# A fused attention and mixture-of-experts layer on one core: values one key tile at a time, shared-expert products in the odd steps, and two orders turned round

## The reference

```python
def holo_linear(x, basis, phase, amp):
    resonance = jnp.einsum('bli,hi->blh', x, basis)
    w = amp * jnp.cos(phase)
    return jnp.einsum('blh,oh->blo', resonance, w)
...
    attn = jnp.einsum('bhqd,bhkd->bhqk', q, k) * scale
    attn = jax.nn.softmax(attn, axis=-1)
    out = jnp.einsum('bhqk,bhkd->bhqd', attn, v)
    out = out.transpose(0, 2, 1, 3).reshape(Bsz, Ls, C)
    return holo_linear(out, basis_o, phase_o, amp_o)
...
    return jax.nn.silu(x @ wg) * (x @ wu) @ wd          # the shared expert
...
x = L0_attn_x
xn = _layernorm(x, axis=-1)
x = x + _L0_attn_ref(xn, ...) + _L0_ffn_ref(xn, ...)
```

## Time and profile before

| | |
|---|---|
| median of 3 runs | 955.16 us (954.87 to 955.76) |
| the profiled execution | 955.04 us, of which the profile's span is 953.2 us |
| TensorE matmul busy | 869.6 us, 91% of the span |
| VectorE, ScalarE, GpSimd busy | 615.2, 577.1 and 402.1 us |
| mean granted TensorE clock | 0.968 of full speed |

### The profile page before, as it was taken

How to read it: one execution, slowest core, us unless ns; L and a number is a source line. 1 busy time by engine, 2 the same in 40 slices (tenths; PEclk the granted TensorE clock), 3 DMA queues, 4 the chain that set the end, 5 groups by cost and what they waited for, 6 DMA issues and landing times.

```text
span 953.2 us, 19558 instructions
## 1 busy us (share of the span) xinstructions
PE 869.6 (91%) x6491; PEld 607.5 (64%) x6492; DVE 615.2 (65%) x923; ACT 577.1 (61%) x935; POOL 402.1 (42%) x411
## 2 busy tenths in 40 slices
PE   4755899999999989889999999999999999999996
PEld 2435899999999976455555556555555555455462
DVE  7788844344434455776786686786786786786752
ACT  4746644444444452766766666766766766766764
POOL 2003322222222151752753752762753753753841
PEclk9865999999999999999999999999999999999998
DMA  9993655222222217454765764765765755745310
GB/s 304 393 287 137 214 151 169 75 72 74 69 69 74 66 48 182 147 169 107 196 177 121 191 179 111 199 181 117 201 172 125 195 173 126 193 132 120 90 39 32
DMA packets 91480, 140.04 MB, mean 147 GB/s; under 512 B 17512, under 2 KB 51824, under 8 KB 89488
## 3 DMA queue, kind: packets, MB, share of 16 engines
q1 hardware_dynamic: 84720, 121.24, 45.2%
q0 software_dynamic: 6480, 17.70, 6.9%
q10 hardware_dynamic: 208, 0.14, 0.1%
HBM read 79.24 MB, written 54.71 MB: 141 GB/s over the span
## 4 chain that ended last, share of the span: by engine, by line
PE 71%; DVE 13%; DMA 7%; issue 3%; SPq 3%; ACT 3%; POOL 0%; DVEq 0%; ACTq 0%
PE bank L1414 9%; PE bank L1454 9%; PE bank L1313 8%; PE s_pair L1366 7%; PE s_pair L1295 7%; PE bank L1519 7%; PE st_pair L1295 6%; DVE top L1886 5%; PE st_pair L1442 5%; DMA r_rows<-low_rank_rows 5%; PE bank L1303 2%; PE bank L1278 2%; PE bank L1427 1%; PE bank L1468 1%; SPq L558 1%
## 5 line engine op out<-in xcount | busy, mean ns | idle before, releaser
L1886 DVE TENSOR_REDUCE top<-s_pair 128x2 f32<-128x1024 f32 x248 | 303.7, 1225 | 141.5 <-PE s_pair L1366 138.0
L1083 ACT ACTIVATE prob<-st_pair 128x1024 f32<-128x1024 f32 x252 | 258.7, 1027 | 123.7 <-PE st_pair L1442 116.8
L756 POOL DMA_INDIRECT xg<-xn_rows,token_of x71 | 73.0, 1028 | 219.6 <-PE bank L1278 168.4
L1414 PE MATMUL bank<-xT_b,w_sh 64*128 64x512 f32 x960 | 144.1, 406 | 0.5
L1366 PE MATMUL s_pair<-k_rows,q_rows 48*128 48x512 f32 x496 | 115.3, 458 | 12.5 <-DVE top L1886 12.3
L1454 PE MATMUL bank<-prob,v_ones 128*32 128x512 f32 x1024 | 123.1, 598 | 0.0
L1414 PEld LDWEIGHTS bank<-xT_b,w_sh 64*128 64x128 f32 x960 | 92.2, 189 | 31.6 <-issue 8.3
L1442 PE MATMUL st_pair<-q_rows,k_rows 50*128 50x512 f32 x504 | 106.3, 416 | 3.4 <-ACT prob L1083 2.5
L1313 PE MATMUL bank<-w_exp,c_hT 128*128 (+1 forms) x639 | 94.2, 292 | 0.6 <-ACT c_y L995 0.6
L1366 PEld LDWEIGHTS s_pair<-k_rows,q_rows 48*128 48x128 f32 x496 | 47.5, 185 | 64.0 <-DVE top L1886 54.3
L794 POOL TENSOR_TENSOR ao<-ao,o_sum 128x512 f32<-128x512 f32 x15 | 19.3, 1286 | 161.2 <-DMA o_sum<-inverse_rows 161.2
(11 more groups left out here) (230 smaller groups left out, 1269.1 us busy)
## 6 DMA issues: line engine op xcount, KB each, us to landing
qk_rows<-qk_hi SPq DMA_DIRECT2D x56, 256.0 KB
q_rows<-qk_rows SPq DMA_DIRECT2D x64, 192.0 KB
k_rows<-qk_rows SPq DMA_DIRECT2D x56, 192.0 KB
expert_rows<-c_y SPq DMA_DIRECT2D x71, 128.0 KB, 1.7
xn_T_split<-x_T SPq DMA_DIRECT2D x8, 1024.0 KB, 6.5
xT_b<-xn_T_split SPq DMA_DIRECT2D x7, 1024.0 KB, 8.8
qk_rows<-qk_lo SPq DMA_DIRECT2D x28, 256.0 KB
x_all<-in_L_attn_x_dram SPq DMA_DIRECT2D x8, 512.0 KB, 8.2
```

The lines of the kernel that those rows point to most:

```text
L756: pool.indirect_dma_start(xg[s % 4][:, :], None, xn_dram, bass.IndirectOffsetOnAxis(token_of[:, s:s + 1], 0)).then_inc(c_x[s % 4], 16)
L1083: act.activation(prob[n % 3][:, 2 * jp:2 * jp + 2, :].rearrange("p j l -> p (j l)"), score_T_pair(b, g, t)[:, :], ACT.Exp, scale=HD ** -0. ...
L1414: ins = pe.matmul((g_bank, u_bank)[up][:, :], w_sh[rows, a, o:o + P], xT_of(b)[rows, c, k, :], start=(n == 0 and i == 0), stop=(n == 1 and ...
L1886: dve.tensor_reduce(top[g % 2][:, :, jp, qt], score_pair(b, g, v)[:, :].rearrange("p (i k) -> p i k", i=2), AX_X, ALU.max).then_inc(d_max, 1)
```

## The change

The change moves work within the pipeline; nothing is computed otherwise.

1. `values` is issued for one key tile in each even step: key tile 3 of the slot before at t = 0, tiles 0, 1 and 2 at t = 2, 4 and 6. Before it came in twos, at t = 0 and t = 4. The semaphore `b_pv` counts every key tile.
2. A gate/up tile has two pieces of six products, at t % 4 = 1 and 3. Before it had 5, 1, 1 and 5, with the single ones at t % 4 = 2 round `small`. A down product has pieces of 12, 5, 12 and 5, at t % 4 = 1, 2, 3 and 0, in place of 10, 5, 5, 12 and 2, and its banks swap once in place of twice.
3. `score_T` comes ahead of `score` in every step. Before this held for t % 4 = 0 alone.
4. `load_low_rank` is issued ahead of `load_rows`.

```diff
@@ SyncE @@
                 if there(nb):
                     load_max(nb, ng)
+                if g == 3 and there(b + 2):
+                    load_low_rank(b + 2)
                 if there(rb):
                     load_rows(rb, rg)
-                if g == 3 and there(b + 2):
-                    load_low_rank(b + 2)
...
             def slot_first():
                 load_max(0, 0)
                 store_low_rank(1)
+                load_low_rank(1)
                 load_rows(0, 2)
-                load_low_rank(1)
@@ ScalarE @@
-                wait(act, b_pv, (b - 1) * 8 + (half + 1) * 4)
+                wait(act, b_pv, (b - 1) * 16 + (half + 1) * 8)
...
-                    wait(act, b_pv, (n - 3) // 2 + 1)
+                    wait(act, b_pv, n - 2)
...
-                wait(act, b_pv, b * 8 + g * 2 + 2)
+                wait(act, b_pv, b * 16 + g * 4 + 4)
@@ TensorE @@
-            CUTS = (0, 5, 6, 7, 12)
-            DOWN_CUTS = (0, 10, 15, 20, 32, 34)
+            CUTS = (0, 6, 12)
...
-                if kt % 2:
-                    ins.then_inc(b_pv, 1)
+                ins.then_inc(b_pv, 1)
...
-            FROM_LAST = len(DOWNS) - 2
-            DOWN_ORDER = [(0, i) for i in range(FROM_LAST)] + [(1, i) for i in range(len(DOWNS))] + [(0, i) for i in range(FROM_LAST, len(DOWNS))]
+            DOWN_ORDER = [(n, i) for n in range(2) for i in range(len(DOWNS))]
+            DOWN_CUTS = (0, 12, 17, 29, 34)
...
-            def piece(b, g, t, n):
+            def piece(b, g, t):
                 what, c, j = unit(b, g, t // 4) if t % 4 else unit_before(b, g, t // 4)
-                if t % 4 == 0:
-                    if what == "down":
-                        down_pair(c, j, 4)
-                elif what == "pair":
-                    gate_up_shared(c, j, n)
...
+                if what == "down":
+                    down_pair(c, j, (t - 1) % 4)
+                elif what == "pair" and t % 2:
+                    gate_up_shared(c, j, t % 4 // 2)
...
                 for t in range(STEPS):
-                    if t % 4:
-                        next_score(b, g, t)
                     if now:
                         score_T(b, g, t)
+                    next_score(b, g, t)
                     if t % 4 == 0:
-                        next_score(b, g, t)
-                        piece(b, g, t, 4)
+                        piece(b, g, t)
                     if t == 0 and there(pb):
-                        values(pb, pg, 2)
                         values(pb, pg, 3)
-                    if t == 4 and now:
-                        values(b, g, 0)
-                        values(b, g, 1)
+                    elif t % 2 == 0 and t:
+                        values(b, g, t // 2 - 1)
...
             low_rank_o(LAST, (0,))
-            values(LAST, 3, TPB - 2)
             values(LAST, 3, TPB - 1)
```

More of the change, by code:

```diff
@@ L1506, in down_pair @@
                         wait(pe, d_res, b)
-                if piece in (2, 4):
-                    pe.wait_ge(b_ha, swaps(b, SFT + 2 * pair) + piece // 2)
+                if piece == 2:
+                    pe.wait_ge(b_ha, swaps(b, SFT + pair) + 1)
                 for m in range(first, end):
@@ L1649, in _ @@
             pe.wait_ge(c_hed, NS)
-            for n in range(3):
-                gate_up_shared(0, 0, n)
+            gate_up_shared(0, 0, 0)
             score(0, 1, 1)
-            gate_up_shared(0, 0, 3)
+            gate_up_shared(0, 0, 1)
             score(0, 1, 2)
@@ L1656, in _ @@
             score(0, 1, 3)
-            for n in range(4):
+            for n in range(2):
                 gate_up_shared(0, 1, n)
```

27 lines of the change are left out of this document (10 added, 17 removed).

## The result

| | before | after |
|---|---|---|
| median | 955.62 us (952.11 to 959.23, 20 runs) | 959.80 us (955.49 to 966.68, 20 runs) |
| ratio | | 1.0047, interval 1.0032 to 1.0061 |
| profiled execution, span | 955.04, 953.2 us | 958.77, 956.9 us |
| TensorE matmul busy | 869.6 us, 91% | 865.0 us, 90% |
| mean granted TensorE clock | 0.968 | 0.964 |

A forecast was written before the change was run, and what follows sets the result against it. TensorE was taken as the engine others wait for, with its own waits small (46.8 us ahead of score pairs, 7.7 for `r_rows`). Terms +2.0 - 1.6 - 7.7 - 2.0 - 1.5 = -10.8 us from 955.04 gave 944, range 938 to 953.5.

The forecast's parts named there:

- the clash: VectorE's split cast beside GpSimd's `normalise`, end of half 2: `normalise` would start some 0.5 behind the cast, gaining 1.6 us.
- the last slot: End of sequence 7, bound by exponentials: one key tile ahead of the last exponential, worth 0.5 plus about 1.0: -1.5 us.
- low-rank rows: TensorE's waits for `r_rows`: with these loads issued ahead, the seven loads' waits fall away, -7.7 us.
- steps, seven sequences: Halves of a sequence sum to -0.45 - 0.03 + 0.45 + 0.3 = +0.3 us, or +2 for seven sequences.
- held step: t = 0 or 4 behind a pair half: ScalarE's exponential holds the next transposed pair, 2.28 us between bounds 2.2 and 2.4.
- The pair half: Four steps in the new order, 2.00, 1.92, 2.00 and 2.28, sum 8.20 us; halves 0 and 1 gain 0.45.
- rivals of dearer or cheaper held steps: Dearer (12%): 2.4 and products wait 0.1 more, +9, 953 us. Cheaper (10%): 2.1 and odd steps 1.9, some -9, 935.
- The odd half: Half 3, bound by VectorE: 9.33 us before, 9.78 new, a loss of 0.45 as TensorE idles.
- Down halves: Halves 4 to 7: 34.96 us before, 35.27 together after, a loss of 0.3; down half 4 at 8.83.
- More switches: Tiling-mode changes from `values` to a projection: no drain beyond 0.01 seen; by the drain rule, 50 changes, +5 us, 949.
- the slower rival: Casts held beside GpSimd (10%): each 1.0 hold costs 0.97, 24 places, +23 us, 967; from 12 on it decides.
- the 8% rival of a new wait: Waits for `r_rows` stay (8%): the low half's store or the engines' traffic takes their place, 952 us.

The follow-up runs named there:

- experiment 4: Changed kernel with ScalarE's exponential ahead of `up_half` at t = 0 and 4 behind a pair half: 957.64 us, ratio 1.0032.
- experiment 5: Changed kernel with `values` in twos again in the last slot of the last sequence: 959.50 us, ratio 1.0052.
- experiment 1: Kernel before with only the low-rank loads moved ahead: 947.88 us, ratio 0.9938; changed kernel with the old load order: 962.99 us, 1.0085.
- steps alone: Changed kernel with the low-rank loads back behind `load_rows`, so only the step changes remain: 962.99 us, ratio 1.0085.
- spread in one half: New order in half 1 alone, on the kernel before with low-rank loads ahead: 944.35 us; the same with the new product pieces everywhere: 944.64 us.
- GpSimd told to wait: Changed kernel with GpSimd's `normalise` and experts' sum waiting until `split_max` is done: 958.81 us, ratio 1.0039.
- split away from GpSimd: Changed kernel with four small `tensor_reduce` and a `memset` in place of the maxima split's cast and subtraction: 955.81 us, ratio 1.0004.

## Why the prediction was wrong

I predicted -10.8 us; the profiled execution shows +3.7. More than half of the miss of 14.5 is one term, the clash (8.0); the last slot has 3.0 and the steps 2.5. Term by term, with two terms that the prediction did not have. Prices of steps are from the sequences without a clash:

| term | predicted | measured | from |
|---|---|---|---|
| low-rank rows | -7.7 | -7.9 | the six waits of the kernel before, 6.6 in their steps, and 1.3 of the half-speed place behind the longest |
| steps, seven sequences | +2.0 | +4.5 | 0.4 in sequence 0, 70.25 - 69.55 = 0.7 in each of 1 to 5 and, for now, in 6 |
| clash | -1.6 | +6.4 | 8.5 - 2.1 |
| sequences 6 and 7 | -2.0 | -1.5 | sequence 6 at +0.1 for +0.7, three slots of 7 at -1.0 |
| last slot and tail | -1.5 | +1.5 | 26.1 - 24.6, from the slot's first transposed pair |
| half-speed place of the changed kernel | none | +1.5 | 4.56 + 3.38 - 3.73 - 2.73 |
| start of the pipeline | none | -0.7 | 380.4 for 381.1, ahead of what was changed |
| sum | -10.8 | +3.8 | trace: +3.7 |

- **What bounds the kernel.** Right: the score pairs' waits did go away (46.8 to 12.4, though these are the weight loads', and the matmuls had waited 8.6). Right too that this alone buys nothing, since a held step takes their place.
- **The pair half.** 8.20 predicted; the measured steps are 1.97, 1.98, 1.96 and 2.26, together 8.17. The held step was 2.28 against 2.26. That ScalarE sets it is shown by experiment 4. Behind a split of the maxima the half has 0.1 more, which I had put at nothing ("nearly no cover left"). The rivals of dearer or cheaper held steps are out; the cheaper one was also priced wrong, for 0.18 and twice 0.1 in 40 halves make 15 us and not 9.
- **The odd half.** 9.78 predicted, 622.27 to 632.09 = 9.82 measured.
- **Down halves.** Here the terms were mis-sized. Down half 4: t = 2 at 2.73 for 2.52, t = 4 at 2.38 for 2.31; a lone key tile costs 0.99 to 1.00 and not half of 1.86, and half-row products behind a full-row projection 0.12 more than in a run. A price read from a group of two had what a group costs beyond its tiles in it once, and half of that was put on each tile.
- **More switches.** I had found "no drain beyond 0.01" between `values` and a projection, and weighed the drain rule at 949. That was a misreading of my own row. The matmuls of `values` start in sets of four. The four sets of the earlier trace rows start at 612.51, 612.97, 613.40 and 613.83, and the next matmul at 614.37: steps of 0.46, 0.43, 0.43 and 0.54. So the way out of the group costs 0.11, and within it the way in 0.02, which I had spread over the two tiles as 1.86; the lone key tile of the changed kernel has the same 0.45 and 0.54. The page TensorEngine Tiling of the Trainium skill (Key Properties) says that a change of the tiling mode drains TensorE, and the 0.11 agrees with that; that it is the drain was not tried by itself. At 0.07 a tile in the nine or ten places of a sequence where it stands on the path that is some 5 us, an estimate, and as much as I had worked out for the rule. Half of it was won back, as steps 1 and 3 came out at 1.97 and 1.96 in place of 2.00.
- **The clash.** This is the step that failed. I wrote that "`normalise` should start some 0.5 behind the cast: a gain of 1.6". In sequence 1, from whose rows I had worked that out, it came true: 0.13 ahead of the cast before, 0.37 behind it now, and nothing is held. But the shift was another in each sequence. It was 1.0 and 0.3 in sequences 2 and 4, where the hold went too, 0.2 and nothing in 5 and 6, where it stayed, and in sequence 3 `normalise` moved the other way, from 0.27 behind the cast to 0.05, and meets the subtraction. I had not thought of that as a second target, though the trace of the kernel before shows it in two of the five sequences that I had counted, here sequence 4:

```profile
690.82 0.17 DVE L1893 CAST top_parts<-top 128x16 fp32r<-128x16 f32 x1
690.90 1.28 POOL L794 TENSOR_TENSOR ao<-ao,o_sum 128x512 f32<-128x512 f32 x1 [1.81 <-DMA o_sum<-inverse_rows]
691.03 1.18 DVE L1895 TENSOR_TENSOR top_parts<-top,top_parts 128x16 fp32r<-128x16 f32 x1
```

The two make a stretch of 0.38 that can be hit. I had moved VectorE by the step lengths and left GpSimd where it was, though the slower rival that I wrote down said itself that eight steps shift the one against the other. That rival (10%) is what happened, in eleven places of halves 0 and 2, where I had said that from 12 on it decides; half 6 had none. Its price of 0.97 was too high: the mean is 0.75 (8.3 over eleven), as some of the hold runs out in the slack of t = 4.
- **The last slot.** -1.5 predicted, +1.5 measured; experiment 5 gives 1.8 of it back in its trace. I counted the key tile that stands ahead of the last exponential, but not that with one tile per step `values` comes up right behind the exponential that makes it. In slots before the last there is a slot's work between them.
- **The loads.** Right in place and size; the 8% rival of a new wait is out. In the new steps the order is worth 3.2 us in medians and 0.4 in the steps, since they hide the wait by themselves (experiment 1); so the full 7.7 could not be credited to the loads on top of the steps, though the whole change does lose the wait.
- **The range** of 938 to 953.5 missed 959.8: 0.10 for slower was too little for a case in which one term alone (the clash) had a spread of 25 us.

Still open: 1.5 of the 3.2 us between steps alone and the changed kernel, and why the clock was lower in some of the runs than in others.

## What to carry to other kernels

Spreading work evenly over steps pays only where the emptied step is longer than the chain of another engine that runs beside it, and the filled step had idle time; find these places by the step lengths and change those alone (one half of eight gained 3.5 us here, and all eight together lost 11.9). Before moving a step by some tenths, list the short instructions of one engine that stand within a microsecond of a long one on the engine that shares its memory port, and count both sides of the shift; moving the short ones to a form that doesn't contend gave 4 us here, a wait for them 1. Price a tile from a group of the size in which it will be issued, and don't add up edits that were measured apart: here the parts sum to +33 us and together cost 12.

## What the runs showed of the hardware

**Half-speed stretches in a busy kernel.** Between 400 and 940 us most executions have a few places at which the granted clock reads 0.50. In the changed kernel, by windows (us busy of TensorE matmul, its weight loads, VectorE, ScalarE and GpSimd, then the granted clock):

```profile
702.00:704.00 2.00, 1.54 (x14) 1.26 (x16) 1.92 (x3) 1.05 (x2) 1.92 (x3) 0.85 0.65 188
704.00:706.00 2.00, 2.00 (x19) 1.65 (x16) 0.68 (x1) 0.00 (x0) 1.19 (x2) 0.50 0.93 269
```

The clock (2.4 GHz at 1.00, 1.2 at 0.50) falls behind the odd half, where TensorE has idled for VectorE, and the two steps there take 4.56 and 3.38 in place of 3.73 and 2.73: 1.5 us. Just ahead of it TensorE had no matmul in flight for 0.82 and then for 0.43. In the kernel before the one such place, at 530 us, follows the longest wait for `r_rows`, 2.09:

```profile
530.00:531.00 1.00, 1.00 (x8) 0.80 (x6) 0.93 (x1) 0.50 (x2) 0.01 (x1) 0.50 0.33 59
```

The profiled executions have between none (spread in one half) and four of these (steps alone, GpSimd told to wait), at some 1.5 us each; the one with the split away from GpSimd has three, the first twice as long and 2.3 us dear. Most of them lie in or just behind an odd half, which the new order made longer. So an idle TensorE may cost twice; that the number follows from the idle time was not tried by itself.

The mean granted clock of every execution is known. Over 211 of them, each set against the mean of its own kernel and series, a clock lower by 0.001 goes with 0.64 us more (correlation -0.76, so over half of the scatter). The estimates in the text above are this price times the difference of the median clocks.

**A held instruction is held to the other's end.** In the changed kernel casts of 0.17 became 0.47 to 1.83 and subtractions 1.17 to 1.29, by how much of the GpSimd operation beside them was left. An instruction with one of its two inputs in PSUM, `qk_lo`, kept its 0.68 throughout.
